# Cross-attention layer: the exponentials of all key tiles added up on GpSimd, and a new table of dense work between the score steps

## The reference, cut to what matters

```python
# x: (16, 224, 512); ctx_1024: (16, 750, 512)
def _L0_xattn_ref(Q, K, V, Wq, bq, Wk, bk, Wv, bv, We, be):
    q = (Q @ Wq + bq).reshape(B, L, 16, 32)
    k = (K @ Wk + bk).reshape(B, S, 16, 32)
    v = (V @ Wv + bv).reshape(B, S, 16, 32)
    scores = jnp.einsum('blhe,bshe->bhls', q, k)
    A = jax.nn.softmax(scale * scores, axis=-1)
    out = jnp.einsum('bhls,bshd->blhd', A, v).reshape(B, L, 512)
    return out @ We + be
x = _layernorm(x + _L0_attn_ref(x, ...))
x = _layernorm(x + _L0_xattn_ref(x, ctx_1024, ctx_1024, ...))     # this layer
x = _layernorm(x + _L0_ffn_ref(x, ...))
```

## Time and profile before

| | us |
|---|---|
| median of 3 runs | 5482.36 |
| lowest, highest | 5481.67, 5484.12 |
| the profiled execution | 5477.36 |
| its span, first to last instruction | 5475.4 |

### The profile page before, as it was taken

How to read it: one execution, slowest core, us unless ns; L and a number is a source line. 1 busy time by engine, 2 the same in 40 slices (tenths; PEclk the granted TensorE clock), 3 DMA queues, 4 the chain that set the end, 5 groups by cost and what they waited for, 6 DMA issues and landing times. The chain is left out here.

```text
span 5475.4 us, 83861 instructions
## 1 busy us (share of the span) xinstructions
PE 3870.9 (71%) x30253; PEld 2713.8 (50%) x30283; DVE 2829.8 (52%) x4238; ACT 1760.5 (32%) x3704; POOL 654.2 (12%) x490
## 2 busy tenths in 40 slices
PE   0499411394169999999999954888835599999960
PEld 0234311262046656666666633656515487878850
DVE  6766888897524444444444436777772122223224
ACT  0105079783023333333333321444411122232210
POOL 0000000000002222222222220000001301000113
PEclk9999555556579999999999986999965799999985
DMA  3001422232121001001001011000001222212213
GB/s 119 0 0 44 116 77 82 79 94 72 59 65 35 23 27 40 23 23 44 23 23 44 8 61 28 0 0 0 0 0 54 89 68 67 70 65 72 68 53 129
DMA packets 156402, 266.11 MB, mean 49 GB/s; under 512 B 75824, under 2 KB 75824, under 8 KB 155264
## 3 DMA queue, kind: packets, MB, share of 16 engines
q1 hardware_dynamic: 143488, 229.39, 13.1%
q0 software_dynamic: 12672, 33.07, 2.1%
HBM read 165.11 MB, written 67.96 MB: 43 GB/s over the span
## 5 line engine op out<-in xcount | busy, mean ns | idle before, releaser
L1393 DVE TENSOR_REDUCE arena<-psum 112x4 f32<-112x1504 f32 x256 | 441.4, 1724 | 768.7 <-PE psum L1223 768.6
L1137 POOL TENSOR_TENSOR arena<-arena 125x896 f32<-125x896 f32 x192 | 401.8, 2092 | 1255.1 <-ACT arena L1366 1255.1
L1366 ACT ACTIVATE arena<-psum 125x1792 f32<-125x1792 f32 x192 | 320.1, 1667 | 400.5 <-PE psum L1236 400.5
L2082 PE MATMUL psum<-tokens_T_high,w_high 128*128 128x224 f32 x1280 | 358.1, 280 | 29.8 <-PE psum L2084 14.9
L543 PE MATMUL psum<-arena 64*112 64x224 bf16 x1024 | 127.3, 401 | 348.7 <-DVEq L652 261.4
L2083 PE MATMUL psum<-tokens_T_rest,w_high 128*128 128x224 f32 x1280 | 354.5, 277 | 0.0
L2084 PE MATMUL psum<-tokens_T_high,w_rest 128*128 128x224 f32 x1280 | 353.9, 276 | 0.0
L668 ACT ACTIVATE arena<-arena,scales 112x224 bf16<-112x224 int8 x512 | 286.0, 559 | 35.3 <-DVEq L653 35.2
L2201 DVE TENSOR_TENSOR gelu_T_rest<-arena,gelu_T_high 128x448 fp32r<-128x448 f32 x160 | 100.1, 625 | 369.7 <-ACT gelu_T_high L2165 369.7
L2160 ACT ACTIVATE arena<-psum 128x448 f32<-128x448 f32 x160 | 87.0, 544 | 633.9 <-PE psum L2084 633.8
L543 PEld LDWEIGHTS psum<-arena 64*112 64x112 bf16 x1024 | 81.8, 200 | 394.4 <-DVEq L652 283.8
(11 more groups left out here) (297 smaller groups left out, 8818.4 us busy)
## 6 DMA issues: line engine op xcount, KB each, us to landing
arena<-L_ffn_moe_w SPq DMA_DIRECT2D x16, 2048.0 KB, 12.2
arena<-arena SPq DMA_DIRECT2D x32, 896.0 KB, 6.1
arena<-ctx SPq DMA_DIRECT2D x16, 1500.0 KB
expert_rows<-arena SPq DMA_DIRECT2D x40, 448.0 KB, 3.1
arena<-x SPq DMA_DIRECT2D x2, 7168.0 KB, 22.5
arena<-x_after_attn SPq DMA_DIRECT2D x32, 448.0 KB, 15.3
dots_ints<-arena SPq DMA_DIRECT2D x16, 784.0 KB, 4.8
arena<-dots_ints SPq DMA_DIRECT2D x16, 784.0 KB, 5.5
```

The source lines that it names most:

```text
L1137: G.tensor_tensor(pair2[:, t, :, :], prob[:, t, :, 0:NS], prob[:, t, :, NS:2 * NS], ALU.add).then_inc(paired, 1)
L1366: S.activation(prob[:, t, :, :], score_psum(MC, 2 * NS), ACT.Exp, scale=SCALE2).then_inc(exp_done, 1)
L1393: return V.tensor_reduce(rmx[:, i // 2, i % 2, :], score_psum(HALF, HC), axis=AX.X, op=ALU.max).then_inc(r_free, 1)
L2082: PE.matmul(to, wh(k), xh(k), start=(k == 0), stop=False)
```

## The change

**The sums.** GpSimd keeps one running sum a group (`folded`, two of them by turns): one addition at t = 0, two each at t = 1 and t = 2, in place, each waiting for the one before it. TensorE then needs one `sums` a group. It stands in the next group, behind slot 1, ahead of `row_max` 1. `attend` moves on VectorE from ahead of the steps to behind slot 2 of t = 0.

**The maxima.** The last eight matmuls of `scores` (224 columns each) become four of 448 columns, which read the same 224 columns twice.

**The table.** K 6 and K 7 of a batch are no longer made in the batch before, but in its own first group (KL). Four of the six VV are cut in two: VA has nine of the twelve matmuls and stands in an odd slot, VB has the other three and stands in the even slot behind it. The C units go from six of group 0's slots to three, and C 6 and C 7 to group 1. No slot is empty any more.

```diff
-        pair2 = sb("exps_of_key_pairs", [MC, TP, GH, NS], F32, L2)
+        folded = sb("exps_over_key_tiles", [MC, 2, GH, NS], F32, L2)
...
+        KL, VA, VB = "k of this batch", "v first part", "v second part"
         SLOTS = (
-            (((C, 0), (C, 1)), ((C, 2), (C, 3)), ((C, 4),), ((O, 0),), ((C, 5),), ((O, 1),), ((C, 6), (C, 7))),
-            (((Q, 0),), ((K, 0),), ((Q, 1),), ((VV, 0),), (), ((K, 1),), ((VV, 1),)),
-            (((K, 2),), ((VV, 2),), ((Q, 2),), ((K, 3),), (), ((VV, 3),), ((K, 4),)),
-            (((K, 5),), ((VV, 4),), ((Q, 3),), ((VV, 5),), (), ((K, 6),), ((K, 7),)),
+            (((KL, 6),), ((KL, 7),), ((C, 0), (C, 1)), ((O, 0),), ((C, 2), (C, 3)), ((O, 1),), ((C, 4), (C, 5))),
+            (((K, 0),), ((VV, 0),), ((C, 6), (C, 7)), ((K, 1),), ((Q, 0),), ((VA, 1),), ((VB, 1),)),
+            (((VV, 2),), ((K, 2),), ((Q, 1),), ((VA, 3),), ((VB, 3),), ((K, 3),), ((Q, 2),)),
+            (((K, 4),), ((VA, 4),), ((VB, 4),), ((VA, 5),), ((VB, 5),), ((K, 5),), ((Q, 3),)),
         )
...
                         for g in range(NG2):
+                            n = b * NG2 + g
+                            ch = Chain(pool, fch, n * (2 * TP - 2))
+                            to = folded[:, g % 2, :, :]
+                            pool.wait_ge(sum_mm, n + 1)
                             for t in range(TP):
-                                i = (b * NG2 + g) * TP + t
-                                pool.wait_ge(exp_done, i + 1)
-                                pool.wait_ge(sum_mm, i + 1)
-                                G.tensor_tensor(pair2[:, t, :, :], prob[:, t, :, 0:NS], prob[:, t, :, NS:2 * NS], ALU.add).then_inc(paired, 1)
+                                pool.wait_ge(exp_done, n * TP + (t + 1))
+                                if t == 0:
+                                    ch.link(G.tensor_tensor(to, prob[:, t, :, 0:NS], prob[:, t, :, NS:2 * NS], ALU.add))
+                                    pool.sem_inc(folds, 1)
+                                else:
+                                    ch.link(G.tensor_tensor(to, to, prob[:, t, :, 0:NS], ALU.add))
+                                    if t < TP - 1:
+                                        ch.link(G.tensor_tensor(to, to, prob[:, t, :, NS:2 * NS], ALU.add))
+                                        pool.sem_inc(folds, 1)
+                                    else:
+                                        G.tensor_tensor(to, to, prob[:, t, :, NS:2 * NS], ALU.add).then_inc(folds, 1)
...
-                    for s in range(2):
-                        for j in range(GH):
-                            rows = slice(DH2 * j, DH2 * (j + 1))
-                            last = PE.matmul(psum[0:MC, j, s * NS:(s + 1) * NS], onesb[rows, 0:MC], mxT[rows, :], start=False, stop=(s == 1))
+                    for j in range(GH):
+                        rows = slice(DH2 * j, DH2 * (j + 1))
+                        last = PE.matmul(psum[0:MC, j, 0:2 * NS], onesb[rows, 0:MC], mxT[rows, :].unsqueeze(1).broadcast_to([DH2, 2, NS]),
+                                         start=False, stop=True)
...
-                def sums(n, g, t):
-                    pe.wait_ge(paired, n * TP + (t + 1 + TP))
+                def sums(n, g):
+                    pe.wait_ge(folds, n * TP + 2 * TP)
...
                         slot(0)
-                        if not (first and g == 0):
-                            sums(n - 1, (g - 1) % NG2, TP - 1)
                         for t in range(TP):
                             next_scores(t)
                             slot(2 * t + 1)
+                            if t == 0 and not (first and g == 0):
+                                sums(n - 1, (g - 1) % NG2)
                             next_max(t + 1)
                             slot(2 * t + 2)
                             next_values(t)
...
                         slot(0)
-                        if not (first and g == 0):
-                            attend(n - 1, (g - 1) % NG2, ch)
...
                         for t in range(TP):
                             slot(2 * t + 1)
                             if more:
                                 reduce_max(n + 1, t + 1)
                             slot(2 * t + 2)
+                            if t == 0:
+                                if not (first and g == 0):
+                                    attend(n - 1, (g - 1) % NG2, ch)
```

More of the change, by code:

```diff
@@ L1022, in decoder_kernel @@
             for slot in SLOTS[g]:
-                ORDER.extend(slot)
+                ORDER.extend(what for what in slot if what[0] != VB)
         assert len(ORDER) % 2 == 0
@@ L1028, in present @@
         def present(unit, first, last):
-            return unit[0] == M or (unit[0] == O and not first) or (unit[0] != O and not last)
+            return unit[0] == M or (unit[0] in (O, KL) and not first) or (unit[0] not in (O, KL) and not last)
         def bank(unit):
-            return 4 + ORDER.index(unit) % 2
+            return 4 + ORDER.index((VA, unit[1]) if unit[0] == VB else unit) % 2
         def earlier_in_bank(unit, first, last):
@@ L1172, in unit @@
                               lambda k: x1T_h[:, k, :], lambda k: x1T_l[:, k, :]).then_inc(q_mm, 1)
-                    elif kind == K:
+                    elif kind in (K, KL):
                         pe.wait_ge(c_rest, b * NC2 + MT)
@@ L1178, in unit @@
                               lambda k: ctxT_h[:, k, keys], lambda k: ctxT_l[:, k, keys]).then_inc(k_mm, 1)
-                    elif kind == VV:
+                    elif kind in (VV, VA, VB):
                         pe.wait_ge(c_rest, b * NC2 + MT)
                         keys = slice(i * MC, (i + 1) * MC)
-                        three(psum[0:MC, at, :], lambda k: ctxT_h[:, k, keys], lambda k: ctxT_l[:, k, keys],
-                              lambda k: Wh["v"][:, k, :], lambda k: Wl["v"][:, k, :]).then_inc(v_mm, 1)
+                        done = three(psum[0:MC, at, :], lambda k: ctxT_h[:, k, keys], lambda k: ctxT_l[:, k, keys],
+                                     lambda k: Wh["v"][:, k, :], lambda k: Wl["v"][:, k, :],
+                                     {VV: range(KC), VA: range(KC - 1), VB: range(KC - 1, KC)}[kind])
+                        if kind != VA:
+                            done.then_inc(v_mm, 1)
                     else:
@@ L1197, in emptied @@
                         pe.wait_ge(q_moved, b * NG2 + (i + 1))
-                    elif kind == K:
+                    elif kind in (K, KL):
                         pe.wait_ge(k_moved, b * (2 * NG2) + (i + 1))
-                    elif kind == VV:
+                    elif kind in (VV, VA):
                         pe.wait_ge(v_moved, b * MT + (i + 1))
@@ L1209, in dense @@
                         return
[L1210 to L1216, removed]
+                    ours = {M: (b, u), KL: (b, u), O: (b_before, 1 - u)}
+                    if kind != VB:
+                        before, back = earlier_in_bank(what, first, last)
+                        if before is not None and back:
+                            emptied(*before, b)
+                        elif before is not None:
+                            emptied(*before, ours.get(before[0], (b_next, 1 - u))[0])
+                    b_unit, u_unit = ours.get(kind, (b_next, 1 - u))
+                    unit(kind, i, bank(what), b_unit, u_unit)
                 def row_max(m, u, g, i):
@@ L1246, in values @@
                     last.then_inc(av_mm, 1)
-                def sums(n, g, t):
-                    pe.wait_ge(paired, n * TP + (t + 1 + TP))
+                def sums(n, g):
+                    pe.wait_ge(folds, n * TP + 2 * TP)
                     for j in range(GH):
-                        last = PE.matmul(psum[DH2 * j:DH2 * (j + 1), 6 + g % 2, NS:2 * NS], ones[0:MC, 0:DH2], pair2[:, t, j, :],
-                                         start=False, stop=(t == TP - 1))
+                        last = PE.matmul(psum[DH2 * j:DH2 * (j + 1), 6 + g % 2, NS:2 * NS], ones[0:MC, 0:DH2], folded[:, g % 2, j, :],
+                                         start=False, stop=True)
                     last.then_inc(sum_mm, 1)
@@ L1294, in next_values @@
                             values(u, g, t)
-                            if t >= 1:
-                                sums(n, g, t - 1)
                         next_max(0)
@@ L1322, in final @@
                 def final():
-                    sums(NB * NG2 - 1, NG2 - 1, TP - 1)
+                    sums(NB * NG2 - 1, NG2 - 1)
                     for i in range(2):
@@ L1358, in slot @@
                                 if present(what, first, last):
-                                    unit(*what, bank(what), b + 1, 1 - u)
+                                    if what[0] == KL:
+                                        unit(*what, bank(what), b, u)
+                                    else:
+                                        unit(*what, bank(what), b + 1, 1 - u)
```

28 lines of the change are left out of this document (14 added, 14 removed).

## The result

| | before | after |
|---|---|---|
| median of 14 runs, us | 5482.95 | 5493.37 |
| lowest, highest | 5471.8, 5486.53 | 5485.14, 5504.76 |
| ratio, with its 95% interval | | 1.0022 (1.0014 to 1.003) |
| span of the profiled execution | 5475.4 | 5486.8 |

The kernel became 10.4 us slower, 0.22%, right at the 11 us that the prediction took for the smallest difference to tell.

A forecast was written before the change was run, and what follows sets the result against it. TensorE's queue was taken as the bound. Loop -3, first batch -5, last batch +7 and clock +5 make +4 on the profiled 5477.4, so 5481; the median lies 5.0 above, so 5486, range 5450 to 5513.

The forecast's parts named there:

- rival A: GpSimd does not hold the combine as forecast: 5469 if only the bias addition's part falls away, 5450 if all; chance 0.22.
- The two terms of the hold: VectorE's combine, ahead of M: held 1.15 us by GpSimd's second addition; in group 3 another 2.4 by the bias addition.
- O 0's: Group 0: O 0 waits 2.0 us for `attend`, now behind the second read of maxima and two rest parts.
- Term 2: End of group 3: the next batch's bias addition on GpSimd meets L1398 or L1400, so M comes 2.4 us later.
- Batch 0: First batch: loses two K pieces (4.5 us), leaves three exponentials uncovered, has its share of groups 1 and 2: -5 us.
- The clock: TensorE's granted clock drops to its lower level after some of the new longer waits: +5 us (0 to +40).
- rival C: Slower: the clock falls in each batch's first group, at O 0 and M of group 3: 5511 us; chance 0.23.
- Group 0: A batch's first group, M to M: 28.4 us against 25.03 before, with O 0's wait of 2.0 in it.
- The last batch: Batch 15: two K pieces +2.3, holds of M +2.5, last `sums` waiting one addition more +2.2: +7 us.
- Group 3: A batch's last group: 25.7 us with the bias addition's hold, also at a turn's end; before 25.74, there 28.7.
- B: The wide matmuls of the maxima cost half: 18 us less at most, 5468; chance 0.10.
- D: Hand-overs on TensorE mispriced, 0.05 us on each of 26 pieces a batch: 20 us either way; only widens the forecast.

The follow-up runs named there:

- hold_off: The changed kernel, with GpSimd's last addition of a group waiting until VectorE has made the next group's negated maxima: 5444.44 us, ratio 0.9939 to the kernel before.
- bias_moved: The changed kernel, with GpSimd's bias addition moved from behind group 3's last addition to behind the t = 0 addition of its batch's first group: 5469.44 us, ratio 0.9981.
- sums_early: The changed kernel, with `sums` put back ahead of the group's first `scores` and `attend` between VectorE's first two reads of maxima: 5462.97 us, ratio 0.9971.
- one_input: The changed kernel, with the combine's first instruction a reduction with one SBUF input instead of an elementwise maximum of two: 5492.33 us, ratio 1.0023.
- wide_only: The kernel before, with only the eight matmuls of the negated maximum turned into four of 448 columns: 5482.03 us, ratio 1.0005.
- attend_first: The changed kernel, with VectorE doing `attend` right behind the second read of maxima, ahead of the C units' rest parts: 5497.31 us, ratio 1.0037.
- old_table: The changed kernel with the `SLOTS` table of the kernel before; sums on GpSimd, wide matmuls and late `attend` stay: 5515.61 us, ratio 1.0061.
- hold_off_sums_early: The changed kernel, with GpSimd's last addition waiting for the combine, and `sums` and `attend` put back to their earlier places: 5419.76 us, ratio 0.9889.

## Why the prediction was right, and where not

**Right by its own steps.** The forecast was 5486 within 5472 to 5500; the median is 5493. The mechanism stood nearly as written: the 0.6 us waits for the maxima go, M and O 0 wait in their place, and the saved work does not arrive. Group 1 was put at 24.4 and measures 24.4, group 2 24.45 and 24.5, group 3 25.7 and 25.4 to 25.5 in seven of the eight batches where no turn ends. M waits 0.81 and 0.33 at the end of groups 1 and 2, where 0.9 and 0.4 were forecast (rival A), and O 0 waits 1.84 where 2.0 was. These are rows of the timeline after, M at the end of groups 0, 1 and 2 of one batch:

```profile
2469.16 0.26 PE L1166 MATMUL psum<-identb,arena 112*128 112x112 bf16 x2 [0.95 <-DVE arena L1418]
...
2493.56 0.26 PE L1166 MATMUL psum<-identb,arena 112*128 112x112 bf16 x2 [0.81 <-DVE arena L1418]
...
2518.01 0.26 PE L1166 MATMUL psum<-identb,arena 112*128 112x112 bf16 x2 [0.33 <-DVE arena L1418]
```

The two terms of the hold, inferred then, are now shown by hold_off (49 us under 5493, 45 by the two ratios to the kernel before) and bias_moved (24, or 22), O 0's by sums_early (30, or 28). The changed kernel itself has the counter-test once: in batch 1 the bias addition starts 0.30 us later than elsewhere (1817.82, behind an addition that ends at 1817.53), when L1417 has begun (1817.59). L1417 takes 0.18, M waits 0.33, and group 3 is 23.3 us.

**Not as written.** Term 2 has one of L1398 and L1400 (now L1416 and L1418) meet the bias addition, and takes L1399 (now L1417) for free, with its one SBUF input. L1416 met the second addition, and the one that met the bias addition was L1417; L1418 never did (0.19 to 0.20 throughout). The size is the same 2.4 us whichever is held, as one_input shows, where L1417 meets the addition and L1418 the bias. So the term came out right though it named the wrong instruction, and that much of it is luck. A small slip: from the end of GpSimd's instruction to that of L1400 are 0.46 us by the two times given, not 0.48.

**Mis-sized.** *Batch 0*: -5 forecast, +0.2 measured. The group that was to gain 3 us lost 2.6 (26.1 against 23.5). Its timeline shows `scores` at 1.87 us instead of 1.04 and `row_max` at 1.61 instead of 0.90, each behind a wait:

```profile
1619.72 1.87 PE L1249 MATMUL psum<-arena 32*125 32x224 f32 x16 [1.54 <-DVE arena L1411]
...
1623.72 1.61 PE L1240 MATMUL psum<-arena 32*112 32x376 f32 x8 [1.76 <-ACT arena L1384]
```

The granted clock is 0.73 there on average (1617.8 to 1643.9), and 0.86 over the same stretch in the kernel before. I had priced the uncovered exponentials and not that TensorE is at the lower clock for longer. *The clock*: +5 forecast for fourteen batches. Group 0 is 27.8 to 28.0 in the loop's first three batches, where the granted clock stays at 1.00; in the other eleven it falls to 0.50 for 3.4 us in the group or from just ahead of it, and the group is 28.6 to 29.5. The mean is 28.9; against the shortest that is 1.1 a batch, 15 us, less the 5 (25.4 against 25.0) that the kernel before also lost. So about 10: rival C's mechanism is there at a third of its price. It was in the right place, the group behind the waits. *Group 0* itself was put at 28.4 without the clock and is 27.8, 8 us the other way. *The last batch*: +7 forecast, +8. *Group 3* was put at 25.7 throughout and is 26.7 where a turn ends, the loop's own wait being 2.9 to 3.5 us there, and less elsewhere; against the kernel before, which has six such ends in these batches and not seven, that is 3 us too little.

These errors are +5 for batch 0, +5 for the clock, -8 for group 0, +3 for group 3 and +1 for the last batch. With 1 us more from group 2 and the start of the layer they make the 7 us between 4 and the 11.4 by which the spans differ. In the fourteen batches of the loop they nearly cancel (+2.4 measured, +2 forecast), which is luck.

**Rivals.** A falls with hold_off: the hold is there in full. B falls with wide_only. C is a third true, as said. Of D little is left, for groups 1 and 2 came within 0.05 us of the sum.

**Open.** When the lower clock comes is not settled. After M's wait of 2.5 us it came in all six batches of the loop in the changed kernel, and in three of six in attend_first. Behind O 0's wait of 1.84 us it never came in the changed kernel, and in five of fourteen batches in hold_off. Why old_table lost 16 us more than I had worked out was not followed up; the trace says only where: 19 us in the fourteen batches, where 12 were expected, 2 in batch 0 and 11 in the last, where 6 were.

## What to carry to other kernels

Before moving work to GpSimd, look what VectorE does from SBUF in the same microseconds: the addition was hidden in GpSimd's own row, and its cost lay in a 0.17 us instruction of VectorE that gates TensorE. A wait that keeps the two apart, ordering the long addition behind the short gate, gave 0.8%, 45 us. Taking work off the engine that bounds pays only where that engine does not wait for another in the next step: the same additions that cost time in old_table gave 45 us in hold_off_sums_early, with the new table laid and both new waits out of the way.

## What the runs showed of the hardware

- A VectorE instruction on eight elements a partition lasted as long as what was left of GpSimd's (1.16 for 0.17, 2.36 for 0.18), with two SBUF inputs as well as with one and a constant; a reduction with one SBUF input did not (0.17 beside GpSimd, in one_input).
- Of three VectorE instructions in a row the first was held by one GpSimd instruction and the second by the next. The first ended 0.02 us after GpSimd's addition (2436.92 and 2436.90); GpSimd's next started at 2436.93, VectorE's next at 2436.95, and that one was held for the whole of it.
- Four bf16 matmuls of 448 columns take the same 0.30 us to the next piece as eight of 224, side by side in four row groups (wide_only).
- In hold_off, with M's 2.5 us wait gone, group 0 was 29.5 us in four of the eight batches with no turn's end ahead and 27.8 in the other four, with the granted clock at 0.50 for 3.4 us in the former and at 1.00 throughout in the latter. In sums_early, with O 0's wait gone, it was 27.5 and 26.0. Either wait alone was enough in some batches.
